# Row maxima of an attention kernel: turned on VectorE in 32x32 blocks instead of on TensorE

## The chip, the cores and the metric

The kernel runs on one core of one Trainium2 chip. Its engines are PE (TensorE, matrix products, with PEld for its weight loads), DVE (VectorE), ACT (ScalarE), POOL (GpSimd) and SP (SyncE, which here only issues DMAs). They run in parallel, each through its own queue in order, and meet in semaphores. The metric is the device time of one execution in microseconds (us).

## The reference

A pre-norm transformer layer on x of 4 sequences, 2048 tokens, 256 features, in float32:

```
h = layernorm(x)
Q, K, V = h Wq^T, h Wk^T, h Wv^T         # 16 heads of 16 features, Q and K turned by RoPE
scores = Q K^T / 4, causal mask           # per sequence and head, 2048 x 2048
x = x + (softmax(scores) V) Wo^T
x = x + relu(layernorm(x) w1 + b1) w2 + b2
```

## The kernel before

There are three stages. Stage 1 normalizes, projects and rotates, and writes q and k (float16, in a high and a low part) and v to scratch in HBM. Stage 2 is the attention, and most of the time. Stage 3 projects the attention's output and does the feed-forward part.

Stage 2 has 16 iterations (4 sequences by 4 groups of 4 heads). An iteration walks 40 steps. A step is one block of 128 keys against one chunk of 512 queries for all 4 heads: chunk 0 has steps 0 to 3, chunk 1 steps 4 to 11, chunk 2 steps 12 to 23, chunk 3 steps 24 to 39. The last four steps of each chunk (0 to 3, 8 to 11, 20 to 23, 36 to 39) lie on the causal diagonal, and their score tiles are 512, 384, 256 and 128 queries wide.

The softmax needs a maximum per query, and since the scores are computed transposed (keys on partitions), the kernel puts minus the maximum in as an extra row (row 48 of each head's 64) of the score product's moving operand `aq`. So each step has two kinds of products:

- Score tiles (L723): one per head, from `ak` and `aq`. ACT takes their exponential into `prob` (L868), POOL zeroes the part above the diagonal in diagonal steps (L898), and PE multiplies with v (L742), one step later.
- Max pairs (L706): two per step, each of two heads. They are approximate scores the other way round, from `mq` and `mk`, half an iteration (LAG = 20 steps) ahead of use. DVE reduces them along the row: one reduction for a full pair (L797), one masking reduction per head on the diagonal (L804). They use four PSUM banks in turn, so that a pair can be written while the pair before it is read.

When the last max pair of a chunk has been read, its row maxima are made ready. This happens in step 24 (for chunk 0 of the next iteration), step 0 (chunk 1), step 4 (chunk 2) and step 20 (chunk 3). DVE reduces the partial maxima to 128x16 (L812), PE transposes them to 16x128 (L714) into a PSUM bank of the max pairs, two uses of the bank ring being counted for it, DVE scales and casts them out (L819), and SP issues four DMAs (L619) that copy them into the four rows of `aq`. PE waits for these rows at the start of steps 0, 4, 12 and 24 (L762). So between the making and the use of the rows lie 16, 4, 8 and 4 steps.

SP's queue in an iteration i is in this order: store of the last output chunk of i-1 (L626, which waits for ACT), rows of chunk 1 (L619), the operands `aq` and `ak` of i+1 (L107, 12 DMAs) and v (L610), rows of chunk 2, sums (L632), two stores, reciprocal sums (L637), the max operands of i+2 (L96, 8 DMAs), rows of chunk 3, a store, rows of chunk 0 of i+1. DMAs of one queue share their engines in order.

In the last 20 steps of the last iteration there are no max pairs left to do.

Of the kernel before, what the change touches and what calls it, by code (L numbers as in the profile page):

```python
# [523 lines left out]
def stage2(nc, x, qk_d, v_d, att_d, rinv_d, weight_ds, weights, ops):  # L524
    with ExitStack() as ctx:
# [6 lines left out]
        ident, mask = ops.ident, ops.mask  # L532
# [3 lines left out]
        qmax = sb("s2_qmax", [P, NC, G * TPC], F32)  # L536
        nrow = sb("s2_nrow", [G * TPC, NC, P], F16)
# [30 lines left out]
        def rows_after(t):

            return [(t // NS, c) for c in range(NC) if t % NS == MAX_END[c]] if t % NS else \  # L570
                [(t // NS - 1, c) for c in range(NC) if t > 0 and MAX_END[c] == NS]

        rows_before = [0]
        for t in range(STEPS_M + 1):
            rows_before.append(rows_before[-1] + len(rows_after(t)))

        def m_use(t, j):

            return G * t + j + ROWS_TILES * rows_before[t]

        def rows_use(i, c):

            t = NS * i + MAX_END[c]
            return G * min(t + 1, STEPS_M) + ROWS_TILES * (rows_before[t] + rows_after(t).index((i, c)))

# [14 lines left out]
        RANK = [sum(e < MAX_END[c] for e in MAX_END) for c in range(NC)]  # L600

# [674 lines left out]
```

## Time and profile before

| | |
|---|---|
| median of 3 runs | 2168.51 us (2166.9 to 2168.56) |
| the profiled execution | 2172.91 us, of it 2171.2 us span from first to last instruction |
| PE busy | 2008.1 us (92%), mean granted clock 0.967 |
| DVE busy | 1902.2 us (88%) |
| ACT, POOL busy | 1457.4 us (67%), 637.1 us (29%) |
| stage 2 | about 227 to 1753 us |

The profiled execution is 4.4 us above the median. A busy PE is not PE at its peak, since its products are pipelined and their ends are modelled: what a step costs on PE is better read from the start of its first product to the start of the next step's. A granted clock of 1.00 is 2.4 GHz, 0.50 is 1.2 GHz.

### The profile page before, as it was taken

The page shows a single profiled execution, that of the slowest core. Times are in us where ns is not written, and L with a number is a line of the kernel's source. Part 1 is how long each engine was busy: PE and PEld are TensorE (multiplying, and loading weights), DVE is VectorE, ACT ScalarE, POOL GpSimd, SP SyncE. Part 2 cuts the span into 40 slices and gives each one's busy share as a digit, 9 for nine tenths or more (in the row PEclk, how much of TensorE's full clock was granted, in tenths as well). Part 3 has the DMA queues.
Part 4 walks back from the last instruction along what each step waited for, and adds up shares of the span by engine and source line. Part 5 has one row for each costly group of instructions (what it writes and reads, how often), then busy time and mean ns, then how long its engine had stood idle before and what let it go on. Part 6 is the DMA issues. An engine that isn't in the chain of part 4 may idle for free. (4 is left out here: it accounts for less than half of the span.)

```text
span 2171.2 us, 53576 instructions
## 1 busy us (share of the span) xinstructions
PE 2008.1 (92%) x19136; PEld 790.4 (36%) x19136; DVE 1902.2 (88%) x3974; ACT 1457.4 (67%) x3092; POOL 637.1 (29%) x1265
## 2 busy tenths in 40 slices
PE   5786599999999999999999999999999969999999
PEld 3444122222222222222222222222222237766776
DVE  8998899999999999999999999999999337777775
ACT  5664078888888788888888788888887742333222
POOL 7999421120221202221121211212212123332231
PEclk9999599999999999999999999999999889999999
DMA  5567331230313303033130322303120212222220
GB/s 193 203 220 209 122 70 37 51 65 17 72 27 64 61 22 66 21 76 50 33 66 17 76 35 52 66 17 74 27 52 13 69 39 78 82 94 84 87 78 29
DMA packets 126407, 152.64 MB, mean 70 GB/s; under 512 B 17248, under 2 KB 92512, under 8 KB 125920
## 3 DMA queue, kind: packets, MB, share of 16 engines
q1 hardware_dynamic: 126176, 149.67, 26.0%
q8 instruction: 132, 2.16, 0.4%
q14 instruction: 99, 0.81, 0.1%
HBM read 90.12 MB, written 59.24 MB: 69 GB/s over the span
## 5 line engine op out<-in xcount | busy, mean ns | idle before, releaser
L868 ACT ACTIVATE s_prob<-s_ps 128x512 f32<-128x512 f32 (+3 forms) x2560 | 1179.3, 540 | 276.5 <-PE s_ps L723 267.3
L797 DVE TENSOR_REDUCE s_part<-s_ps 128x2 f32<-128x1024 f32 x768 | 909.1, 1222 | 42.7 <-PE s_ps L706 25.1
L742 PE MATMUL s_ps<-s_prob,s_v 128*32 128x256 f32 (+3 forms) x10240 | 744.4, 363 | 8.4 <-POOL s_prob L898 0.9
L723 PE MATMUL s_ps<-aq,ak 64*128 64x512 f16 (+3 forms) x2560 | 674.5, 355 | 7.2 <-DVE s_part L804 1.2
L706 PE MATMUL s_ps<-mk,mq 64*128 64x512 f16 (+3 forms) x2560 | 590.7, 355 | 60.4 <-DVE s_part L797 28.1
L898 POOL TENSOR_SCALAR_AFFINE_SELECT s_prob<-s_prob 128x128 f32<-128x128 f32 x1024 | 286.7, 292 | 1170.7 <-ACT s_prob L868 1158.2
L804 DVE CUSTOM_DVE_ANT_0 s_ps<-s_ps,mask_sb 128x512 f32<-128x512 f32 (+3 forms) x1024 | 472.3, 520 | 25.9 <-PE s_ps L706 20.6
L723 PEld LDWEIGHTS s_ps<-aq,ak 64*128 64x128 f16 x2560 | 180.9, 93 | 524.0 <-ACT s_prob L868 439.9
L742 PEld LDWEIGHTS s_ps<-s_prob,s_v 128*32 128x32 f32 x10240 | 202.2, 108 | 464.4 <-issue 378.3
L706 PEld LDWEIGHTS s_ps<-mk,mq 64*128 64x128 f16 x2560 | 141.0, 95 | 105.4 <-DVE s_part L797 48.9
L1166 ACT ACTIVATE s_h_f<-s_ps,s_b_s 128x512 f32<-128x512 f32 x128 | 87.9, 687 | 105.9 <-PE s_ps L1031 85.0
L804 DVE DVE_READ_ACCUMULATOR2_ANT s_part<- 128x1 f32 x1024 | 145.3, 142 | 0.2
L1041 PE MATMUL s_ps<-w_hi,s_h_hi 128*128 128x256 f16 x512 | 139.6, 273 | 2.0 <-DVE s_h_lo L1106 2.0
L1041 PE MATMUL s_ps<-w_hi,s_h_lo 128*128 128x256 f16 x512 | 139.6, 273 | 0.0
L1041 PE MATMUL s_ps<-w_lo,s_h_hi 128*128 128x256 f16 x512 | 139.6, 273 | 0.0
L1106 DVE TENSOR_TENSOR s_h_lo<-s_h_f,s_h_hi 128x512 f16<-128x512 f32 x128 | 100.0, 781 | 4.4
L140 POOL TENSOR_TENSOR o_in<-o_in,r_in 128x1024 f32<-128x1024 f32 x16 | 38.0, 2376 | 202.9 <-DMA r_in<-rinv_scratch 202.9
L445 POOL TENSOR_TENSOR s_rot_b<-s_rot_b,s_sin 128x512 f32<-128x512 f32 x64 | 92.8, 1450 | 14.0 <-DVE s_rot_b L384 13.9
L447 POOL TENSOR_TENSOR s_rot_a<-s_rot_a,s_rot_b 128x512 f32<-128x512 f32 x64 | 93.7, 1463 | 5.0
L1104 DVE CAST s_h_hi<-s_h_f 128x512 f16<-128x512 f32 x128 | 61.8, 483 | 30.2 <-ACT s_h_f L1166 24.9
L1031 PE MATMUL s_ps<-s_xt_hi,w_hi 128*128 128x512 f16 x256 | 77.1, 383 | 2.7 <-DVE s_xt_lo L1099 2.6
L321 PE MATMUL s_ps<-s_xt_hi,s_w_hi 128*128 128x512 f16 x128 | 43.6, 427 | 38.1 <-DVE s_xt_lo L376 33.6
(86 smaller groups left out, 1562.1 us busy)
## 6 DMA issues: line engine op xcount, KB each, us to landing
v_scratch<-s_vst SPq DMA_DIRECT2D x32, 512.0 KB, 3.9
s_v<-v_scratch SPq DMA_DIRECT2D x16, 1024.0 KB, 10.8
att_scratch<-s_o SPq DMA_DIRECT2D x64, 256.0 KB, 2.4
aq<-qk_scratch SPq DMA_DIRECT2D x96, 128.0 KB, 4.3
ak<-qk_scratch SPq DMA_DIRECT2D x96, 128.0 KB, 6.9
s_xin<-x SPq DMA_DIRECT2D x16, 512.0 KB, 4.4
qk_scratch<-s_r_lo SPq DMA_DIRECT2D x64, 128.0 KB, 2.2
qk_scratch<-s_r_hi SPq DMA_DIRECT2D x64, 128.0 KB, 2.4
```

Of the source, the lines that this page charges most:

```text
L445: nc.gpsimd.tensor_tensor(rot_b[:, g], rot_b[:, g], sin[:, tok], ALU.mult).then_inc(rotsin_done, 1)
L447: nc.gpsimd.tensor_tensor(rot_a[:, g], rot_a[:, g], rot_b[:, g], ALU.add).then_inc(rot_done, 1)
L706: nc.tensor.matmul(ps[:, bank_of(use + jj), 0:w], mq[rows, p, pair, qt * P:(qt + 1) * P], mk[rows, p, pair, kc * CH:kc * CH + w], start=Tr ...
L723: nc.tensor.matmul(ps[:, s_bank(s, j), q0:CH], ak[rows, p, j // 2, kb * P:(kb + 1) * P], aq[rows, p, j // 2, c * CH + q0:(c + 1) * CH], st ...
L742: last = nc.tensor.matmul(ps[32 * j:32 * j + 32, O_BANK, cols], v[:, p, kb, j, :], prob[:, s % 2, j, cols], start=kb == 0 and part == 0, s ...
L797: nc.vector.tensor_reduce(part[:, qt // TPC, :, pair, qt % TPC, kc], ps[:, bank_of(use):bank_of(use) + 2, 0:w], AX.X, ALU.max).then_inc(m_ ...
L804: nc.vector.tensor_tensor_reduce(out=ps[:, bank, 0:w], in0=ps[:, bank, 0:w], in1=mask[:, CH - w:CH], scale=1.0, scalar=MASKED, op0=ALU.add ...
L868: nc.scalar.activation(prob[:, s % 2, j, q0:CH], ps[:, s_bank(s, j), q0:CH], ACT.Exp, scale=1.0 / (SQK * DK ** 0.5)).then_inc(p_done, 1)
L898: nc.gpsimd.affine_select(out=block, in_=block, compare_op=ALU.is_ge, fill=0.0, base=0, pattern=[[1, P]], channel_multiplier=-1).then_inc( ...
L1041: last = nc.tensor.matmul(ps[:, Y_BANK + pair, t * D:(t + 1) * D], a[:, p, k, tt * P:(tt + 1) * P], w[:, k], start=q == 0, stop=q == len(m ...
L1106: nc.vector.tensor_tensor(h_lo[:, p, f], h_f[:, f % 2], h_hi[:, p, f], ALU.subtract).then_inc(hlo_done, 1)
L1166: nc.scalar.activation(h_f[:, f % 2], ps[:, H_BANK + f % 2], ACT.Relu, bias=b1_s[:, f:f + 1], scale=SH / SQK).then_inc(h_done, 1)
```

## The change

The transpose leaves PE and PSUM. `qmax` becomes 128x32 per chunk (its columns 16 to 31 are set to zero once), and DVE turns it in four 32x32 blocks, each in its own 32 partitions, within SBUF (`turn_chunk`, new). The turned maxima of 128 queries stand then in four groups of 16 partitions with 32 queries each, and not in 16 partitions with 128. DVE does reduction, turn and scaling one after the other, between the two max pairs of a step, and each waits for the one before. SP waits for `nrow_done` and issues eight DMAs for a chunk, each for 32 of every 128 queries and two heads: 8 partitions of 64 bytes into one row of `aq`. For this `aq` is laid out with the chunk outside the head pair, so that the eight pieces lie at one step, and its load from scratch becomes twelve DMAs of 64 KB in pieces of 1 KB, where it was six of 128 KB in pieces of 4 KB.

The second part is in the last 20 steps of the last iteration. In the eight diagonal ones of them, PE computes two pairs of products 512 wide into the banks of the max pairs (`filler_pair`, new), which nobody reads; before the first of these 20 steps it waits until DVE has read all max pairs.

```diff
@@ load_a
-                dst = (ops.ak if qk else ops.aq)[rows, p]
-                src = qk_d[...].rearrange("a (jp jj r) t -> (a jj) r jp t", jj=2, r=DK)
-                sp.dma_start(dst, src[jj]).then_inc(ops.a_in[p], 16)
+                src = qk_d[...].rearrange("a (jp jj r) t -> (a jj) r jp t", jj=2, r=DK)[jj]
+                if qk:
+                    sp.dma_start(ops.ak[rows, p], src).then_inc(ops.a_in[p], 16)
+                    continue
+                for jp in range(NP):
+                    sp.dma_start(ops.aq[rows, p, :, jp], src[:, jp].rearrange("r (c t) -> r c t", c=NC)
+                                 ).then_inc(ops.a_in[p], 16)
@@ stage2, sync: rows
-                sp.wait_ge(m_read, NM + rows_use(i, c) + ROWS_TILES)
-                for j in range(G):
-                    row = HROWS * (j % 2) + MAXROW
-                    k = TPC * (NP * (j % 2) + j // 2)
-                    sp.dma_start(aq[row:row + 1, i % 2, j // 2, c * CH:(c + 1) * CH], nrow[k:k + TPC, c, :]
-                                 ).then_inc(rows_in[c], 16)
+                sp.wait_ge(nrow_done, NC * i + RANK[c] + 1)
+                for jj in range(2):
+                    row = HROWS * jj + MAXROW
+                    dst = aq[row:row + 1, i % 2, c].rearrange("a n (q u x) -> a u (n q) x", u=P // TURN, x=TURN)
+                    for u in range(P // TURN):
+                        k = TURN * u + NP * TPC * jj
+                        sp.dma_start(dst[:, u], nrow[k:k + NP * TPC, c, :]).then_inc(rows_in[c], 16)
@@ stage2, tensor
-            def max_rows(i, c):
-                use = rows_use(i, c)
-                pe.wait_ge(qmax_done, NC * i + RANK[c] + 1)
-                pe.wait_ge(m_read, use + ROWS_TILES)
-                nc.tensor.transpose(ps[0:G * TPC, bank_of(use), 0:P], qmax[:, c, :], ident[:]
-                                    ).then_inc(m_ready, ROWS_TILES)
+            def filler_pair(p, s, pair):
+                qt, kc = MAX_TILES[(s + LAG) % NS]
+                for jj in range(2):
+                    rows = slice(HROWS * jj, HROWS * (jj + 1))
+                    nc.tensor.matmul(ps[:, M_BANK + 2 * pair + jj], mq[rows, p, pair, qt * P:(qt + 1) * P],
+                                     mk[rows, p, pair, 0:CH], start=True, stop=True)
...
+                    if t == STEPS_M:
+                        pe.wait_ge(m_read, NM + m_use(STEPS_M, 0))
...
+                    elif is_diagonal(s):
+                        filler_pair(p, s, 0)
@@ stage2, vector
+            def turn_chunk(i, c):
+                dve.wait_ge(qmax_done, NC * i + RANK[c] + 1)
+                nc.vector.transpose(qmax_t[:, c, :], qmax[:, c, :]).then_inc(turned, 1)
...
-                nc.vector.tensor_scalar(nrow[:, c, :], ps[0:G * TPC, bank_of(use), 0:P], -1.0 / SQK, None, ALU.mult
-                                        ).then_inc(m_read, ROWS_TILES)
+                nc.vector.tensor_scalar(nrow[:, c, :], qmax_t[:, c, :], -1.0 / SQK, None, ALU.mult).then_inc(nrow_done, 1)
...
-                    for of, c in rows_after(t):
-                        max_of_chunk(of, c)
+                for i, c in ended(t):
+                    max_of_chunk(i, c)
+                    turn_chunk(i, c)
+                    rows_out(i, c)
```

The order of DVE's instructions in step 0, before (L804 are the masking reductions and their accumulator reads, L812 the reduction of a chunk, L819 the scaling):

```order
L804 ISA s_part 128x1
L812 TENSOR_REDUCE s_qmax<-s_part 128x16 [waits s2_m_read]
L804 ISA s_ps,s_part<-s_ps,mask_sb 128x512 [waits s2_m_ready]
L804 ISA s_part 128x1
L804 ISA s_ps,s_part<-s_ps,mask_sb 128x512 [waits s2_m_ready]
L804 ISA s_part 128x1
L819 TENSOR_SCALAR s_nrow<-s_ps 16x128 [waits s2_rows_in1,s2_m_ready]
```

The same place after the change (L801 masks, L809 reduces, L814 turns, L819 scales):

```order
L801 ISA s_part 128x1
L809 TENSOR_REDUCE s_qmax<-s_part 128x16 [waits s2_m_read]
L814 STREAM_TRANSPOSE s_qmax_t<-s_qmax 128x32 [waits s2_qmax_done]
L819 TENSOR_SCALAR s_nrow<-s_qmax_t 128x32 [waits s2_rows_in1,s2_turned]
L801 ISA s_ps,s_part<-s_ps,mask_sb 128x512 [waits s2_m_ready]
L801 ISA s_part 128x1
```

The scaling has moved ahead of the step's second max pair, behind a new instruction, and waits for DVE itself instead of PE.

SP's queue of one iteration before, from its load of `aq` on:

```order
L107 DMA aq<-qk_scratch 16x2x2048 x6
L107 DMA ak<-qk_scratch 16x2x2048 x6
L610 DMA s_v<-v_scratch 128x16x128
L619 DMA aq<-s_nrow 1x4x128 x4
L632 DMA s_sums<-att_scratch 128x1x64
```

And after it (L110 loads `aq`, L616 copies the rows, L605 loads v):

```order
L110 DMA aq<-qk_scratch 16x4x512 x12
L107 DMA ak<-qk_scratch 16x2x2048 x6
L605 DMA s_v<-v_scratch 128x16x128
L616 DMA aq<-s_nrow 1x8x32 x8
L628 DMA s_sums<-att_scratch 128x1x64
```

Nothing has changed places here, but 17 issues have become 27. PE's queue loses its L714 at the end of steps 0, 4, 20 and 24, and is otherwise as before up to the last 20 steps.

## Rows read from the trace of the kernel before

Columns of a timeline: start us, duration us, engine, line, instruction, output<-inputs, form, count, and in brackets the idle time before it and what ended it. Columns of windows: stretch, its length, busy us (and instructions) of PE, PEld, DVE, ACT and POOL, granted clock of PE, busy share of the DMA engines, GB/s.

**Rows 1.** Timeline of PE: first score products of nine steps of one iteration.
```profile
825.70 0.39 PE L723 MATMUL s_ps<-aq,ak 64*128 64x512 f16 x2
...
834.20 0.39 PE L723 MATMUL s_ps<-aq,ak 64*128 64x512 f16 x2
...
839.70 0.39 PE L723 MATMUL s_ps<-aq,ak 64*128 64x512 f16 x2
...
844.54 0.39 PE L723 MATMUL s_ps<-aq,ak 64*128 64x512 f16 x2
...
852.22 0.39 PE L723 MATMUL s_ps<-aq,ak 64*128 64x512 f16 x2
...
856.97 0.39 PE L723 MATMUL s_ps<-aq,ak 64*128 64x512 f16 x2
...
871.51 0.39 PE L723 MATMUL s_ps<-aq,ak 64*128 64x512 f16 x2
...
880.02 0.39 PE L723 MATMUL s_ps<-aq,ak 64*128 64x512 f16 x2
...
885.51 0.39 PE L723 MATMUL s_ps<-aq,ak 64*128 64x512 f16 x2
```

**Rows 2.** Timeline of PE, end of step 0: the transpose and the wait behind it.
```profile
828.06 0.27 PE L714 MATMUL s_ps<-ident_sb,s_qmax 128*16 128x128 f32 x1 [0.39 <-DVE s_qmax L812]
...
829.33 0.33 PE L706 MATMUL s_ps<-mk,mq 64*128 64x384 f16 x1 [0.32 <-DVE s_part L804]
```

**Rows 3.** Windows while the loads of the next iteration land.
```profile
842.00:844.00 2.00, 2.00 (x24) 0.51 (x21) 2.00 (x2) 1.64 (x4) 0.00 (x0) 1.00 1.03 130
846.00:848.00 2.00, 2.00 (x24) 0.52 (x21) 2.00 (x9) 1.70 (x5) 0.95 (x4) 1.00 1.20 294
```

**Rows 4.** Timeline of DVE: runs of full max pairs, waiting for PE and catching up.
```profile
852.97 12.11 DVE L797 TENSOR_REDUCE s_part<-s_ps 128x2 f32<-128x1024 f32 x10 [0.28 <-PE s_ps L706]
...
865.45 6.90 DVE L797 TENSOR_REDUCE s_part<-s_ps 128x2 f32<-128x1024 f32 x6
```

**Rows 5.** Lines of DVE over the whole span: busy us, mean ns | idle before.
```profile
L812 DVE TENSOR_REDUCE s_qmax<-s_part 128x16 f32<-128x64 f32 x64 | 13.6, 212 | 0.0
L827 DVE RECIPROCAL s_rinv<-s_sums 128x64 f32<-128x64 f32 x15 | 8.1, 543 | 0.0
```

**Rows 6.** Timeline of SP (DMA issues) in the same iteration.
```profile
828.74 0.36 SPq L626 DMA_DIRECT2D att_scratch<-s_o  x1
829.43 2.42 SPq L619 DMA_DIRECT2D aq<-s_nrow  x4
831.90 2.77 SPq L107 DMA_DIRECT2D aq<-qk_scratch  x6
...
837.51 0.62 SPq L610 DMA_DIRECT2D s_v<-v_scratch  x1
838.19 8.94 SPq L619 DMA_DIRECT2D aq<-s_nrow  x4
...
874.22 0.42 SPq L96 DMA_DIRECT2D mk<-qk_scratch  x1
875.25 2.47 SPq L619 DMA_DIRECT2D aq<-s_nrow  x4
```

**Rows 7.** DMA issues, whole span: KB each, median us from issue to landing.
```profile
rinv_scratch<-s_rinv SPq DMA_DIRECT2D x15, 32.0 KB, 1.4
```

**Rows 8.** Windows at two falls of the granted clock.
```profile
1655.00:1660.00 5.00, 4.14 (x36) 1.17 (x36) 4.14 (x15) 3.83 (x9) 2.04 (x7) 0.78 0.14 53
1660.00:1665.00 5.00, 4.91 (x69) 1.66 (x61) 3.90 (x21) 2.78 (x10) 2.46 (x9) 0.88 0.00 0
1715.00:1720.00 5.00, 5.00 (x30) 0.93 (x29) 0.00 (x0) 3.64 (x7) 0.00 (x0) 0.50 0.61 171
```

**Rows 9.** Timeline of PE, last iteration: first score products of steps 25 and 32.
```profile
1710.66 1.29 PE L723 MATMUL s_ps<-aq,ak 64*128 64x512 f16 x3
...
1734.33 0.79 PE L723 MATMUL s_ps<-aq,ak 64*128 64x512 f16 x3
```

More of the change, by code:

```diff
@@ L530, in sem @@
             return ctx.enter_context(nc.semaphore(name))
-        ident, mask = ops.ident, ops.mask
+        mask = ops.mask
+        TURN = 32
         mq, mk, aq, ak, m_in, a_in = ops.mq, ops.mk, ops.aq, ops.ak, ops.m_in, ops.a_in
@@ L535, in stage2 @@
         part = sb("s2_part", [P, NC, 2, NP, TPC, NC], F32)
-        qmax = sb("s2_qmax", [P, NC, G * TPC], F32)
-        nrow = sb("s2_nrow", [G * TPC, NC, P], F16)
+        qmax = sb("s2_qmax", [P, NC, TURN], F32)
+        qmax_t = sb("s2_qmax_t", [P, NC, TURN], F32)
+        nrow = sb("s2_nrow", [P, NC, TURN], F16)
         prob = sb("s2_prob", [P, 2, G, CH], F32)
@@ L566, in stage2, with ended @@
         STEPS_M = NIT * NS
[L568 to L575, printed above, removed]
+        RANK = [sum(e < MAX_END[c] for e in MAX_END) for c in range(NC)]
+        def ended(t):
+            return [(i, c) for i in (t // NS - 1, t // NS) for c in range(NC)
+                    if 0 <= i < NIT and t == NS * i + MAX_END[c]]
         def m_use(t, j):
[L579 to L584, printed above, removed]
+            return G * t + j
         def bank_of(use):
@@ L598, in read_before @@
             return ST * i + last_in_bank + 1
-        RANK = [sum(e < MAX_END[c] for e in MAX_END) for c in range(NC)]
         def crosses_diagonal(qt, kc):
@@ L723, in score_tile @@
                 nc.tensor.matmul(ps[:, s_bank(s, j), q0:CH], ak[rows, p, j // 2, kb * P:(kb + 1) * P],
-                                 aq[rows, p, j // 2, c * CH + q0:(c + 1) * CH], start=True, stop=True
+                                 aq[rows, p, c, j // 2, q0:CH], start=True, stop=True
                                  ).then_inc(s_ready, 1)
@@ L771, in iteration @@
                         max_pair(t, 1)
+                    elif is_diagonal(s):
+                        filler_pair(p, s, 1)
                     value_step(i, p, s, 1)
-                    if t <= STEPS_M:
-                        for of, c in rows_after(t):
-                            max_rows(of, c)
             for t in range(LAG):
@@ L779, in _ @@
                     max_pair(t, pair)
-                for of, c in rows_after(t):
-                    max_rows(of, c)
             for u in range(NIT // 2):
@@ L809, in max_of_chunk @@
             def max_of_chunk(i, c):
[L811 to L813 removed]
+                dve.wait_ge(m_read, NM + m_use(NS * i + MAX_END[c], 0))
+                nc.vector.tensor_reduce(qmax[:, c, 0:G * TPC], part[:, c].rearrange("p j n q k -> p (j n q) k"), AX.X,
+                                        ALU.max).then_inc(qmax_done, 1)
+            def turn_chunk(i, c):
+                dve.wait_ge(qmax_done, NC * i + RANK[c] + 1)
+                nc.vector.transpose(qmax_t[:, c, :], qmax[:, c, :]).then_inc(turned, 1)
             def rows_out(i, c):
[L816 to L817 removed]
+                dve.wait_ge(turned, NC * i + RANK[c] + 1)
                 dve.wait_ge(rows_in[c], 16 * ROWS_DMAS * i)
[L819 to L820 removed]
+                nc.vector.tensor_scalar(nrow[:, c, :], qmax_t[:, c, :], -1.0 / SQK, None, ALU.mult).then_inc(nrow_done, 1)
             def invert_sums(i):
@@ L832, in step @@
                     max_of_pair(t, 0)
-                if t <= STEPS_M:
-                    for of, c in rows_after(t):
-                        max_of_chunk(of, c)
+                for i, c in ended(t):
+                    max_of_chunk(i, c)
+                    turn_chunk(i, c)
+                    rows_out(i, c)
                 if t < STEPS_M:
                     max_of_pair(t, 1)
-                if t <= STEPS_M:
-                    for of, c in rows_after(t):
-                        rows_out(of, c)
             dve.sem_inc(m_read, NM)
             nc.vector.memset(part[:], -3e38).then_inc(part_preset, 1)
+            nc.vector.memset(qmax[:], 0.0).then_inc(qmax_preset, 1)
             dve.wait_ge(ops.const_in, 16)
             dve.wait_ge(part_preset, 1)
+            dve.wait_ge(qmax_preset, 1)
             for t in range(LAG):
```

16 lines of the change are left out of this document (5 added, 11 removed).

## The prediction, made before the changed kernel was run

> **What bounds the kernel now.** I read the timeline of PE first and take the start of a step's first score product as its clock. Steps 0, 4, 6, 8, 12, 14, 20, 24 and 26 of one iteration start at 825.70, 834.20, 839.70, 844.54, 852.22, 856.97, 871.51, 880.02 and 885.51 [rows 1]. The reader is to see two lengths for the same work. Four diagonal steps without a transpose take 852.22 - 844.54 = 7.68 us (8 to 11), with one 8.50 (0 to 3) and 8.51 (20 to 23). Two full steps after a diagonal take 856.97 - 852.22 = 4.75 us without, 5.50 (4, 5) and 5.49 (24, 25) with. So a transpose costs 0.82, 0.75, 0.83 and 0.74 us, 3.14 us an iteration, though its own product is 0.27. The rest is waiting: 0.39 us for DVE's reduction before it, and 0.32 behind it in the next max pair, since the transpose takes a turn of the bank ring [rows 2].
>
> Then DVE and PE in a full stretch: both are shown busy for all of 2.00 us [rows 3]. DVE's runs tell them apart. Ten reductions in a row take (12.11 - 1.22) / 9 = 1.21 us each, and when DVE is late after the reciprocal, six take (6.90 - 1.22) / 5 = 1.14 [rows 4]. DVE can go faster than it goes, so PE sets the pace at 2.42 a step and DVE has 0.15 to spare.
>
> Last the queue of SP [rows 6], since rows of maxima reach PE through it and PE waits for them at steps 4, 12 and 24. None of these waits binds now: steps 4 and 24 start without delay against steps 12 and 8 to 11. How near they are is the question.
>
> **PE.** 64 transposes go. Were nothing else late, 16 x 3.14 = 50 us would come back.
>
> **DVE.** Before, a chunk cost the reduction, 0.21 [rows 5], and a scaling. Now it is reduction, turn, scaling, each waiting for the last. No row shows a turn of 128x32 in SBUF. Nearest below is the reduction, 0.21, nearest above the reciprocal of 128x64, 0.54 [rows 5]; I take 0.2 to 0.25 each for turn and scaling, which are smaller than either, so some 0.65 us between the two max pairs, at most 1.3. The reciprocal already puts 0.5 in between full pairs and DVE catches up by itself. In diagonal steps the second pair of the next step can be 0.1 to 0.3 late. I count nothing for it, because the row DMAs below are later still; if they were not, it would be 2 x 0.2 x 16 = 6 us.
>
> A rule on this: the scaling now reads and writes SBUF, and the Trainium skill (SBUF — State Buffer, Who interferes with whom) says that such a VectorE instruction in a two-port mode needs a port pair that it shares with GpSimd, and that whichever comes second is blocked until the other ends. POOL masks in just these diagonal steps. By it the scaling would be late by up to one mask, which hides in the same place; no row here shows the case.
>
> **SP.** This is where the cost is. Four row DMAs take 2.42 us of issue, 0.605 each with the gap [rows 6]; load issues take 0.46 (six in 2.77) and the last operand load 0.42. The new ones are eight per chunk, of the same kind as the old row DMAs (few partitions into one), so I price them at 0.605. Bounds: 0.40, as the store (0.36 and a gap), and 0.65, as the load of v. The landing of a row DMA is not in the trace. From below it is 1.4 us, as for a small store [rows 7]. From above it is 2.9: the fourth issue starts at about 831.25 and PE starts step 4 unhindered at 834.20 [rows 1, 6]. I take 1.6, near the lower row, which is a transfer as small.
>
> The Trainium skill (DMA: Bandwidth & Descriptors, Why a DMA increments its semaphore by 16 and not by 1) says that a DMA is spread over the largest number up to 16 that divides the slowest dimension of both sides, and that the issuing queue writes the missing counts itself. The rows agree in that the copy with 4 partitions takes longer to issue (0.57) than that with 16 (0.42) [rows 6]. By that rule 8 would still be below 16 and pay it, which speaks for 0.605; without it, each would cost 0.46 and the second rival below would hold.
>
> Step 4, times from the start of step 0: the store is issued at 3.04, rows begin at 3.44 (DVE is ready before), the eighth issue starts 7 x 0.605 later at 7.68 and lands at 9.3. PE would be there at 7.68. Steps 0 to 3 take 9.3 instead of 8.50: +0.8.
>
> Step 12: rows of chunk 1 end at 8.28, then 18 loads of 0.467 (there were 12) to 16.7, v to 17.3. Before, the first row DMA of chunk 2 was held: four took 8.94 us from 838.19, so the other three began at about 845.3. The DMA engines were full at 130 GB/s until then and at 294 after [rows 3, 6]. That is 13.4 us after the first load issue at 831.90. The same bytes at the same rate from 8.28 on give 21.7, seven more issues have the last start at 25.3, and it lands at 26.9. PE would reach step 12 at 9.3 + (852.22 - 834.20) - 0.75 - 0.4 = 26.2, where 0.4 is what PE recovers after a wait because ACT and POOL have caught up (estimate: the short product with v of step 3 leaves 4.35 of PE's work in two steps, against 4.75). So steps 0 to 11 take 26.9 against 26.52: +0.4 in all.
>
> Step 24, from the start of step 20: the eight operand loads end at 874.64 - 871.51 = 3.13, rows begin at 3.17, the eighth starts at 7.41, lands at 9.0, against 8.51 before: +0.5. Steps 24 and 25: -0.74 - 0.4 = -1.1. Steps 12 to 19 as before.
>
> Sum of an iteration: 0.4 + 0.5 - 1.1 = -0.2, over 16: -3 us. The 50 us are spent on SP.
>
> **Granted clock.** In the trace it fell in stage 2 after the thinnest stretches of PE's work. In 1655 to 1665 it was 0.78 and 0.88, so 5 x 0.22 / 0.5 + 5 x 0.12 / 0.5 = 3.4 us at 1.2 GHz [rows 8]; there are three such falls in stage 2 (the others near 740 and 1200), each in or after eight diagonal steps (36 to 39, 0 to 3) with a transpose's gap. Now PE stands still for 1.3 to 1.6 us at the end of such stretches, 32 times (steps 4 and 24). I expect the clock to fall at 20 of them. With PE as the bound, 3.4 us at half clock lose 1.7: 34 us, of which 0.7 x 10 hides before step 12, less three falls of before: +23.
>
> **The tail.** Without max pairs the clock fell after the diagonal steps 20 to 23 and stayed at 0.50 [rows 8]: steps 25 to 31 took 1734.33 - 1710.66 = 23.67 us [rows 9]. After it seven steps take 15.4 (2.2 each, where PE no longer waits for the clock). The unread products keep PE as busy as elsewhere, so I expect this fall to go: -8.3. They cost some 0.5, and the wait for DVE's last reductions 1.2 (one pair): -6.5. Six more issues at the end of stage 1 hide behind a full DMA queue: up to 2.8, I take 1.
>
> Sum: 2172.9 - 3 + 23 - 6.5 + 1 = 2187.4 for a profiled execution, which stood 4.4 above the median; so 2183.
>
> **Rivals.**
> 1. The rows arrive in time and PE's gain stays (faster). If an issue costs 0.42 and a gap, step 4 opens at 3.44 + 7 x 0.45 + 1.4 = 8.0 and the 0.3 of waiting is recovered. Then 2172.9 - 50 + 6 - 6.5 = 2122, at the median 2118. It decides below 0.5 us an issue. For it: plain loads issue in 0.46. Against: the row DMAs themselves never do. 22%.
> 2. The waits come, the clock holds. 2187.4 - 23 = 2164, at the median 2160. For it: of 48 diagonal groups only three fell. Against: none of them had such a standstill. 25%.
> 3. As forecast, with the falls. 43%; 2165 to 2205 on its own.
> 4. Worse: the halved loads of `aq` in 1 KB pieces drain slower than 130 GB/s, or falls are longer. A quarter more for the `aq` half is 1.5 us at step 12 each time, 24 us: 2207 and up to 2228. 10%.
>
> The range is 2114 to 2225. A measurement of this kernel tells 0.2% (4 us) from no change. Faster: all of 1, most of 2 and a little of 3, 0.40; same 0.10; slower 0.50.
>
> **What would show it.** PE idle before step 4 and step 24 with DMA on `aq` as the releaser, 1 to 2 us, and less before step 12; steps 4 and 5 in 4.4 us; row DMAs at 0.57 each, eight in 4.8 us; more stretches below 1.00 in the granted clock; no stretch at 0.50 from 1711 to 1732. I am wrong if steps 0 to 3 take 7.7 us, or if a row DMA issues in 0.4 us, and wrong in the clock if it stays at 1.00 in spite of the waits.

## The result and the profile after

| | before | after |
|---|---|---|
| median | 2167.88 us (2166.9 to 2168.56, 4 runs) | 2280.27 us (2276.73 to 2287.94, 4 runs) |
| ratio, 95% interval | | 1.0524 [1.0492, 1.0555] |
| span of the profiled execution | 2171.2 us | 2275.2 us |
| mean granted clock | 0.967 | 0.934 |

The change made the kernel 5.2% slower, 112 us. "Slower" was the likeliest of my cases, but the forecast was 2183 us and the range ended at 2225: the loss is over seven times the 15 us that I gave it. The chain that I had drawn is there in the trace: row DMAs late on SP, PE standing still for them, the clock falling behind. Nearly every link of it is longer than I priced it.

Where the 104 us of span are, by step starts: up to step 0 of the first iteration +2.6 us; from there to step 19 of the last iteration +107.6 us; from there to the end -6.2 us. So it is the body of stage 2. A usual iteration of before takes 91.8 us; of after they take 97 to 103.

The longest entry in the waits of PE is new (line waited for, us in total, times, longest us):

```profile
PE s_ps L719 <- DMA aq<-s_nrow: 77.2, 42, 3.1
```

The timeline of PE after shows one iteration, first score products of steps 0, 4, 6, 8, 12, 14, 20, 24, 26 and the next 0 (L719 is now the score product). It answers to [rows 1]:

```profile
867.77 0.39 PE L719 MATMUL s_ps<-aq,ak 64*128 64x512 f16 x2
...
877.70 0.60 PE L719 MATMUL s_ps<-aq,ak 64*128 64x512 f16 x2 [1.60 <-DMA aq<-s_nrow]
...
884.90 0.39 PE L719 MATMUL s_ps<-aq,ak 64*128 64x512 f16 x2
...
889.75 0.39 PE L719 MATMUL s_ps<-aq,ak 64*128 64x512 f16 x2
...
898.34 0.39 PE L719 MATMUL s_ps<-aq,ak 64*128 64x512 f16 x2 [0.87 <-DMA aq<-s_nrow]
...
903.10 0.39 PE L719 MATMUL s_ps<-aq,ak 64*128 64x512 f16 x2
...
917.64 0.39 PE L719 MATMUL s_ps<-aq,ak 64*128 64x512 f16 x2
...
927.32 0.39 PE L719 MATMUL s_ps<-aq,ak 64*128 64x512 f16 x2 [1.33 <-DMA aq<-s_nrow]
...
933.14 0.39 PE L719 MATMUL s_ps<-aq,ak 64*128 64x512 f16 x2
...
965.15 0.39 PE L719 MATMUL s_ps<-aq,ak 64*128 64x512 f16 x2
```

The reader is to see three waits for the row DMAs, at steps 4, 12 and 24. Steps 0 to 3 take 9.93 us (8.50 before), 4 to 11 take 20.64 (18.02), 20 to 23 take 9.68 (8.51). Steps 4 and 5 take 7.20 us where they took 5.50 with a transpose, and 4.75 was to be had: a fall of the clock. Steps 12 and 13 take 4.76, as before, so nothing is recovered after a wait.

The timeline of SP in the same iteration answers to [rows 6] (L616 rows, L110 loads of `aq`):

```profile
870.81 0.36 SPq L622 DMA_DIRECT2D att_scratch<-s_o  x1
871.22 5.40 SPq L616 DMA_DIRECT2D aq<-s_nrow  x8
877.00 7.71 SPq L110 DMA_DIRECT2D aq<-qk_scratch  x12
884.75 2.91 SPq L107 DMA_DIRECT2D ak<-qk_scratch  x6
887.71 0.59 SPq L605 DMA_DIRECT2D s_v<-v_scratch  x1
888.34 8.69 SPq L616 DMA_DIRECT2D aq<-s_nrow  x8
...
920.81 5.43 SPq L616 DMA_DIRECT2D aq<-s_nrow  x8
```

A row DMA takes 5.40 / 8 = 0.675 us to issue (forecast 0.605), a load of `aq` 7.71 / 12 = 0.64 (forecast 0.467). The second group of rows takes 8.69 instead of 5.4, since it is held behind the loads as before, but begins 20.6 us after step 0, not 17.3.

Windows after (columns as in [rows 3]): the first in PE's standstill before step 4, the second while the loads of `aq` are issued, the third when those of `ak` follow, the fourth behind step 24.

```profile
876.00:878.00 2.00, 0.40 (x6) 0.12 (x4) 0.46 (x4) 0.00 (x0) 0.45 (x2) 0.94 0.01 1
878.00:880.00 2.00, 2.00 (x16) 0.47 (x12) 1.14 (x1) 1.57 (x3) 0.00 (x0) 0.50 0.36 94
...
886.00:888.00 2.00, 2.00 (x24) 0.47 (x16) 1.94 (x2) 1.64 (x4) 0.00 (x0) 1.00 1.07 188
...
929.00:931.00 2.00, 2.00 (x18) 0.69 (x21) 1.93 (x6) 2.00 (x5) 0.00 (x0) 0.50 0.00 0
```

Before, the first load of `aq` was issued at 831.90 [rows 6], and these are the windows that follow:

```profile
832.00:834.00 2.00, 1.91 (x39) 0.86 (x35) 1.94 (x12) 1.49 (x7) 1.52 (x6) 1.00 0.52 125
834.00:836.00 2.00, 1.93 (x32) 0.61 (x24) 1.66 (x5) 1.49 (x4) 0.63 (x3) 1.00 1.03 131
```

Two things: PE runs at 1.2 GHz right behind a standstill, and the DMA engines are 0.32 to 0.42 busy at 94 to 111 GB/s for the 7.7 us in which `aq` is loaded. Before, they were full at 131 GB/s 2 us after the first load was issued. SP's issuing has become the limit of the load, so that its bytes end later. Read in windows of 5 us, the clock was low for 188 us from 280 us to the end of stage 2, in 34 falls of 3.4, 6.8 or 10.2 us; before for 31 us in 4 falls, 20.5 of them in the tail.

VectorE's part answers to [rows 5] (lines over the whole span, busy us, mean ns | idle before): reduction, turn, scaling.

```profile
L809 DVE TENSOR_REDUCE s_qmax<-s_part 128x16 f32<-128x64 f32 x64 | 13.5, 211 | 0.0
L814 DVE STREAM_TRANSPOSE s_qmax_t<-s_qmax 128x32 f32<-128x32 f32 x64 | 13.5, 212 | 2.2
L819 DVE TENSOR_SCALAR s_nrow<-s_qmax_t 128x32 f16<-128x32 f32 x64 | 11.6, 181 | 2.2
```

The turn costs 0.21 us and the scaling 0.18; I had priced each at 0.2 to 0.25.

### The profile page after: what moved, and what is told of

Its sections match the earlier page's. It is cut to its first block and busy times, and to the rows that moved or that the text cites. A ratio compares the mean times of both kernels' runs of the same rounds, so it can differ in the third digit from the quotient of the medians.

```text
span 2275.2 us, 53866 instructions
## 1 busy us (share of the span) xinstructions
PE 2066.4 (91%) x19104; PEld 802.1 (35%) x19104; DVE 1912.0 (84%) x4039; ACT 1453.2 (64%) x3092; POOL 637.0 (28%) x1265
## 2 busy tenths in 40 slices
DMA packets 143306, 152.69 MB, mean 67 GB/s; under 512 B 24928, under 2 KB 112480, under 8 KB 142816
## 5 line engine op out<-in xcount | busy, mean ns | idle before, releaser
L719 PE MATMUL s_ps<-aq,ak 64*128 64x512 f16 (+3 forms) x2560 | 709.1, 371 | 84.5 <-DMA aq<-s_nrow 77.2
L738 PE MATMUL s_ps<-s_prob,s_v 128*32 128x256 f32 (+3 forms) x10240 | 762.5, 371 | 7.6 <-ACT s_o L858 3.2
L702 PE MATMUL s_ps<-mk,mq 64*128 64x512 f16 (+3 forms) x2560 | 632.6, 374 | 42.3 <-DVEq L839 19.1
L801 DVE CUSTOM_DVE_ANT_0 s_ps<-s_ps,mask_sb 128x512 f32<-128x512 f32 (+3 forms) x1024 | 466.1, 525 | 9.5 <-PE s_ps L702 8.4
L719 PEld LDWEIGHTS s_ps<-aq,ak 64*128 64x128 f16 x2560 | 186.8, 94 | 640.9 <-ACT s_prob L867 474.9
L702 PEld LDWEIGHTS s_ps<-mk,mq 64*128 64x128 f16 x2560 | 152.8, 96 | 82.6 <-DVE s_part L801 31.0
L801 DVE DVE_READ_ACCUMULATOR2_ANT s_part<- 128x1 f32 x1024 | 142.7, 139 | 0.0
L449 POOL TENSOR_TENSOR s_rot_b<-s_rot_b,s_sin 128x512 f32<-128x512 f32 x64 | 92.8, 1450 | 15.6 <-DVE s_rot_b L388 15.5
```

Source lines behind the costliest of these rows:

```text
L449: nc.gpsimd.tensor_tensor(rot_b[:, g], rot_b[:, g], sin[:, tok], ALU.mult).then_inc(rotsin_done, 1)
L702: nc.tensor.matmul(ps[:, bank_of(use + jj), 0:w], mq[rows, p, pair, qt * P:(qt + 1) * P], mk[rows, p, pair, kc * CH:kc * CH + w], start=Tr ...
L719: nc.tensor.matmul(ps[:, s_bank(s, j), q0:CH], ak[rows, p, j // 2, kb * P:(kb + 1) * P], aq[rows, p, c, j // 2, q0:CH], start=True, stop=T ...
L738: last = nc.tensor.matmul(ps[32 * j:32 * j + 32, O_BANK, cols], v[:, p, kb, j, :], prob[:, s % 2, j, cols], start=kb == 0 and part == 0, s ...
L801: nc.vector.tensor_tensor_reduce(out=ps[:, bank, 0:w], in0=ps[:, bank, 0:w], in1=mask[:, CH - w:CH], scale=1.0, scalar=MASKED, op0=ALU.add ...
```

## The experiments

Theory S: SP's queue, with eight row DMAs a chunk and twelve loads, opens steps 4, 12 and 24 late, and the clock falls behind PE's standstills. Theory T: VectorE's chain, or the new order on it, is what costs.

**e1, the row DMAs alone.** Before, each row DMA cut in two (2 partitions of 256 bytes instead of 4), transposes and loads as they were.

```diff
-                    sp.dma_start(aq[row:row + 1, i % 2, j // 2, c * CH:(c + 1) * CH], nrow[k:k + TPC, c, :]
+                    for h in range(2):
+                        q0 = c * CH + h * CH // 2
+                        sp.dma_start(aq[row:row + 1, i % 2, j // 2, q0:q0 + CH // 2],
+                                     nrow[k + TPC // 2 * h:k + TPC // 2 * (h + 1), c, :]
```

> The kernel before (transpose on TensorE, plain load of aq), with each of its four row DMAs per chunk cut in two, so eight per chunk. Theory S (the row DMAs on SP's queue open steps 4, 12 and 24 late): rows begin 3.7 us after step 0, the eighth issue starts 7 x 0.65 later and lands 1.75 after that, so steps 0 to 3 take about 10.1 us instead of 8.5, steps 20 to 23 about 10.1, steps 0 to 11 some 2 us more in all, and the granted clock falls after the waits; in all 60 to 110 us slower, 2230 to 2280. Theory T (the turn on VectorE and the new order of DVE make the change slow): 2168, no change.

Measured: 2220.48 us, ratio 1.024 [1.0216, 1.0264]. 256 more small DMAs on a queue with no change on VectorE or PE cost 52 us. Steps 0 to 3 and 20 to 23 take 9.5 and 9.6 us, 4 to 11 stay at 18.0, and there are eleven falls of the clock. This is S in kind, but less than its 60 to 110 us, since the steps take 9.5 and not 10.1. Over half of the loss of after is missing.

**e2, the loads alone.** Before, with the new layout of `aq` and its twelve loads in pieces of 1 KB, four row DMAs.

```diff
+                for jp in range(NP):
+                    sp.dma_start(ops.aq[rows, p, :, jp], src[:, jp].rearrange("r (c t) -> r c t", c=NC)
...
-        A_DMAS = 2 * 3 * 2
+        A_DMAS = 2 * 3 * (NP + 1)
```

> The kernel before with only the new layout of aq and its load in twelve DMAs of 1 KB pieces; four row DMAs per chunk as before. Theory S: the load keeps SP 3.5 us longer before the rows of chunk 2, which then land at about 24.5 us after step 0, while PE arrives at 26.5: not late, so 2165 to 2175. Rival L (the longer load alone costs): steps 4 to 11 grow by some 2 us, 2200.

Measured: 2175.47 us, ratio 1.0038 [1.002, 1.0056]; step 12 late seven times, 5.0 us in all. The loads alone take up the slack before step 12 and cost 8 us by the ratio, 6.5 by the medians.

**e11, both together.** Before with the edits of e1 and e2, transposes kept.

> The kernel before, transposes kept, with both changes of SP's queue together: eight row DMAs a chunk (e1) and the new layout of aq with twelve loads (e2). Alone they cost 52 and 8 us. Theory G (each gate is the end of one queue, so the two add up only at step 12, where nothing was late in either alone): from the start of step 0, rows of chunk 1 end at 8.0, twelve loads of 0.64 at 15.7, six of 0.485 at 18.6, v at 19.2, rows of chunk 2 are held to about 23.5, five more of 0.56 and a landing of 1.75 give 28.6, where PE comes at 9.5 + 18.0 = 27.5. So 1.1 us more an iteration than e1 and e2 together, and some falls behind it: 2240 to 2255. Rival A (the costs are independent and add): 2225 to 2232, step 12 on time. If instead it is at 2275 or more, SP's queue sets the time of the kernel after whatever PE and VectorE do, and the transposes' 50 us would show nowhere.

Measured: 2264.78 us, ratio 1.044 [1.0382, 1.0498]: 98 us, where e1 and e2 add to 60. Neither number held; G was right in kind, since step 12 is now late nearly every time. Its waits and one iteration of SP:

```profile
PE s_ps L729 <- DMA aq<-s_nrow: 58.9, 44, 2.4
```
```profile
863.26 4.90 SPq L625 DMA_DIRECT2D aq<-s_nrow  x8
868.53 8.47 SPq L110 DMA_DIRECT2D aq<-qk_scratch  x12
...
880.63 7.70 SPq L625 DMA_DIRECT2D aq<-s_nrow  x8
```

So a queue of SP with as many issues as that of after loses 98 of the 112 us, with PE and VectorE as they were. The kernel after has no transposes and is still 15 us slower than e11, though the two intervals just touch. What PE saves before a wait makes the wait longer: 77.2 us of waits against 58.9. Its row DMAs are also dearer, 5.40 us for eight against 4.90 here; the runs don't tell these two apart.

**e3, the order of SP's queue.** After, with rows of chunk 2 ahead of the loads of the next iteration and rows of chunk 3 ahead of the max operands.

```diff
                 rows(i, 1)
+                rows(i, 2)
                 if not last:
                     ...
                     load_v(i + 1, 1 - p)
-                rows(i, 2)
...
+                rows(i, 3)
                     load_m(sp, ops, qk_d, i + 2, p)
-                rows(i, 3)
```

> The changed kernel with SP's queue in another order: rows of chunk 2 ahead of the loads of the next iteration, rows of chunk 3 ahead of the max operands; still eight row DMAs. Theory S: the wait at step 12 goes (steps 4 to 11 in 17.3 us plus what a fall of the clock costs, instead of 20.3), steps 20 to 23 take 9.1 instead of 9.6, the wait of 1.6 us at step 4 stays: 2190 to 2225. Theory T: 2280.

Measured: 2223.73 us, ratio 1.0255 [1.0232, 1.0278]. With rows no longer behind the loads the waits go from 77.2 to 42.6 us, all of them now at steps 4 and 24 (1.5 and 0.9 us in a usual iteration), and 57 us come back. Half of the loss was the place of the rows in the queue, most of it the gate at step 12 and what hangs on it; the rows of chunk 3, also moved, shorten steps 20 to 23 from 9.68 us to 9.28, some 6 us of the 57. The falls went from 34 to 20.

This trace also prices the falls where no gate at step 12 hides them. Steps 4 to 11 take 17.26 us in the one iteration without a fall behind step 4, and 19.3 to 19.9 in the twelve with one of 6.8 us. The start of steps 4 and 12 in one of these (L719):

```profile
857.58 0.57 PE L719 MATMUL s_ps<-aq,ak 64*128 64x512 f16 x2 [1.52 <-DMA aq<-s_nrow]
...
877.29 0.39 PE L719 MATMUL s_ps<-aq,ak 64*128 64x512 f16 x2
```

Over the sixteen iterations that is 32 us, and 15 more lie between step 24 and the next step 4. An iteration without falls would take 92.4 us, 0.6 more than before. So of the 55 us that e3 is behind the kernel before, falls of the clock account for about 47 (by the lengths of steps, in a single trace).

**e4, four row DMAs.** After, with one DMA for both halves of the heads: 16 partitions of 64 bytes into two rows.

```diff
-                for jj in range(2):
-                    row = HROWS * jj + MAXROW
-                    dst = aq[row:row + 1, i % 2, c].rearrange("a n (q u x) -> a u (n q) x", u=P // TURN, x=TURN)
-                    for u in range(P // TURN):
-                        k = TURN * u + NP * TPC * jj
-                        sp.dma_start(dst[:, u], nrow[k:k + NP * TPC, c, :]).then_inc(rows_in[c], 16)
+                dst = aq[MAXROW:MAXROW + HROWS + 1:HROWS, i % 2, c].rearrange("a n (q u x) -> a u (n q) x", u=P // TURN, x=TURN)
+                for u in range(P // TURN):
+                    sp.dma_start(dst[:, u], nrow[TURN * u:TURN * u + G * TPC, c, :]).then_inc(rows_in[c], 16)
```

> The changed kernel with four row DMAs per chunk instead of eight, each of 16 partitions by 64 bytes into two rows of aq; twelve load DMAs and the order as in the change. Theory S: the fourth issue starts 1.9 us after the first, rows are there 7.1 us after step 0 (PE comes at 7.7) and 6.8 after step 20, and those of chunk 2 just in time; no waits, no falls of the clock behind them, and all of PE's 3.1 us an iteration comes back: 2110 to 2130. Theory T: above 2200.

Measured: 2146.41 us, ratio 0.9898 [0.9873, 0.9924], faster than before. This one edit takes away 134 us. Rows of chunk 1 in SP's timeline:

```profile
822.37 2.15 SPq L613 DMA_DIRECT2D aq<-s_nrow  x4
```

2.15 us instead of 5.40; no wait at steps 4 and 24, nine at step 12 (7.6 us). T is refuted as the cause of the loss: turn, chain and order on VectorE are those of after. But I had expected 2110 to 2130. The iteration took 89.9 us at best, not 91.8 - 3.1 = 88.7, and e6 and e10 show why.

**e6, four row DMAs and the order.** e4 with the order of e3, the load of the sums also ahead of the loads.

```diff
                 rows(i, 1)
+                rows(i, 2)
+                if not first:
+                    load_sums(i - 1)
                 if not last:
```

> The kernel after, with four row DMAs a chunk as in e4, and the order of e3: rows of chunk 2, then the sums, ahead of the loads of the next iteration; rows of chunk 3 ahead of the max operands. Theory S: the last waits for rows (7.6 us at nine steps in e4) go, and with them a few stretches behind them: 2134 to 2142, against 2146 of e4, and no more, because in e4 VectorE had no idle time in the diagonal steps 0 to 3, which took 8.27 us and not the 7.68 forecast: its chain of reduction, turn and scaling (0.62 us) is on the path there, 1.2 us an iteration, 19 us in all. Rival T (the turn on VectorE is harmless, and what keeps e4 from the 50 us is all rows): 2115 to 2125, steps 0 to 3 in 7.7.

Measured: 2133.67 us, ratio 0.9848 [0.9833, 0.9863]. No wait for rows is left, no fall between the first iteration and the end of stage 2, and an iteration takes 89.87 us. Step starts 0, 4, 8 and 12 (L716):

```profile
813.41 0.39 PE L716 MATMUL s_ps<-aq,ak 64*128 64x512 f16 x2
...
821.68 0.39 PE L716 MATMUL s_ps<-aq,ak 64*128 64x512 f16 x2
...
831.28 0.39 PE L716 MATMUL s_ps<-aq,ak 64*128 64x512 f16 x2
...
838.94 0.39 PE L716 MATMUL s_ps<-aq,ak 64*128 64x512 f16 x2
```

Steps 8 to 11 take 7.66 us, steps 0 to 3 8.27. The timeline of DVE in step 0 (L798 masks, L806 to L816 the chain) has no idle time in brackets behind its first line, nor has it any for the rest of the four diagonal steps:

```profile
814.19 0.70 DVE L798 CUSTOM_DVE_ANT_0 s_ps<-s_ps,mask_sb 128x512 f32<-128x512 f32 x1 [0.41 <-PE s_ps L699]
...
815.45 0.21 DVE L806 TENSOR_REDUCE s_qmax<-s_part 128x16 f32<-128x64 f32 x1
815.70 0.21 DVE L811 STREAM_TRANSPOSE s_qmax_t<-s_qmax 128x32 f32<-128x32 f32 x1
815.95 0.18 DVE L816 TENSOR_SCALAR s_nrow<-s_qmax_t 128x32 f16<-128x32 f32 x1
816.11 0.70 DVE L798 CUSTOM_DVE_ANT_0 s_ps<-s_ps,mask_sb 128x512 f32<-128x512 f32 x1
```

**e10, a part of the chain off VectorE.** e6 with the scaling on GpSimd, behind its masks of the same step.

```diff
-                nc.vector.tensor_scalar(nrow[:, c, :], qmax_t[:, c, :], -1.0 / SQK, None, ALU.mult).then_inc(nrow_done, 1)
+                nc.gpsimd.tensor_scalar(nrow[:, c, :], qmax_t[:, c, :], -1.0 / SQK, None, ALU.mult).then_inc(nrow_done, 1)
```

> The kernel of e6 with the scaling of the turned maxima on GpSimd, after its masks of the same step, instead of on VectorE. In e6 VectorE had no idle time in steps 0 to 3 (8.27 us against 7.68 of steps 8 to 11 before), so the 0.18 us of the scaling should be on the path twice an iteration. Theory D (VectorE sets the pace in these steps): steps 0 to 3 and 20 to 23 each 0.15 to 0.2 shorter, 8.1, and 5 to 6 us in all: 2128, ratio to before 0.981. Rival (something else sets 8.27, ACT or the bank ring): 8.27 stays, 2132 to 2135. A second rival, slower: rows come later by GpSimd's queue and PE waits at steps 4 and 24 for over 0.3 us: 2140 or more.

Measured: 2130.96 us, ratio 0.9827 [0.9811, 0.9844]. Steps 0 to 3 and 20 to 23 take 8.03 us, 0.24 less each, an iteration 89.4 to 89.5. That is D, 0.45 us in an iteration. From the first step 0 to step 19 of the last iteration its trace is 5.3 us shorter than that of e6. The medians differ by only 2.7 us, with intervals that overlap: the first step 0 of its trace lies 1.8 us later than in e6. That VectorE sets the pace in these steps is shown by the step lengths; that e10 is faster than e6 is likely, not shown.

**e5 and e9, unread products before the waits.** After, with six unread products on PE just before the wait for rows at steps 4 and 24 (e5), or five there and sixteen at step 12 (e9). They write only into banks that the next max pair overwrites.

```diff
+                    if s in (CHUNK_START[1], CHUNK_START[3]) and t < STEPS_M:
+                        pe.wait_ge(m_read, m_use(t, 0) + 2)
+                        for k in range(6):
+                            ...
+                            nc.tensor.matmul(ps[:, bank_of(m_use(t, 0) + k % 2)], mq[rows, t // NS % 2, 0, 0:P],
+                                             mk[rows, t // NS % 2, 0, 0:CH], start=True, stop=True)
                     if s in CHUNK_START:
                         pe.wait_ge(rows_in[STEPS[s][0]], 16 * ROWS_DMAS * (i + 1))
```

> The kernel after, with six unread products of 512 columns (1.3 us) on PE just before its wait for the rows at steps 4 and 24. The waits are left as they are; PE only does not stand still in them. It tells the price of the clock's falls from the price of the waits. Theory S (rows late on SP, and each standstill of PE after thin diagonal steps lets the clock fall): the falls, 31 in the kernel after, go to under 8, and the steps of a no-fall iteration stay at 95.9 us against 91.8 before; time 2215 to 2235, against 2280. Rival W (the falls have another cause, or cost nothing because they lie in time that is waited for anyway): 2270 to 2290, with 25 or more falls.

> The kernel after, with unread products of 512 columns on PE ahead of all three waits for rows: five (1.1 us) at steps 4 and 24, sixteen (3.4 us) at step 12. In e5 the sum of the waits stayed (78 us), but step 12 still opened 20.2 us after step 4, so that PE stood still there for 2 to 4 us and the clock fell behind it instead. Theory S (the gate at step 12 is SP's and fixed; a fall costs only where no gate follows it): with no standstill left, 5 falls or fewer between the first and the last iteration, iterations of 95.9 to 96.5 us, 2230 to 2245 in all, against 2282. Rival W (the falls come for another reason, or products of this kind don't hold the clock): 15 falls or more and 2270 to 2290.

Measured: e5 2282.39 us, ratio 1.053 [1.0511, 1.055]; e9 2259.29 us, ratio 1.0423 [1.0402, 1.0444]. e5 missed: no time came back, as W had it, although the falls went from 34 to 20 and low clock from 188 us to about 147 (17 of them one fall in the tail). Its step 12 tells why:

```profile
1082.17 0.39 PE L719 MATMUL s_ps<-aq,ak 64*128 64x512 f16 x2 [1.14 <-DMA aq<-s_nrow]
...
1102.34 0.39 PE L719 MATMUL s_ps<-aq,ak 64*128 64x512 f16 x2 [2.83 <-DMA aq<-s_nrow]
```
```profile
1095.00:1100.00 5.00, 4.43 (x67) 1.61 (x59) 4.92 (x26) 3.38 (x12) 3.32 (x12) 1.00 1.06 214
1100.00:1105.00 5.00, 2.66 (x24) 0.73 (x24) 1.25 (x2) 2.10 (x4) 0.00 (x0) 0.77 0.19 64
1105.00:1110.00 5.00, 5.00 (x37) 1.02 (x29) 3.66 (x3) 2.81 (x6) 0.00 (x0) 0.55 0.15 56
```

Step 12 opens 20.17 us after step 4, as in after (20.64), whether PE runs fast or slow in between. A fall behind step 4 is time that would have been waited for at step 12; with that fall gone, PE stands still 2.83 us there and the clock falls behind step 12 instead. In e9 eleven falls are left (55 us of low clock) and 21 us came back, which is between S and W: its iterations without a fall are at 95.3 to 97.1 us, near the 95.9 to 96.5 of S, but the products were too short to fill the waits. Products of two heads run beside each other, so that sixteen took 1.90 us and not the 3.4 I had counted, and 51.5 us of waits remained:

```profile
1382.27 1.90 PE L763 MATMUL s_ps<-mk,mq 64*128 64x512 f16 x16
1385.20 0.39 PE L719 MATMUL s_ps<-aq,ak 64*128 64x512 f16 x2 [1.02 <-DMA aq<-s_nrow]
```

So in the kernel after the clock's share is bounded, not measured: at least those 21 us.

**e7 and e8, the unread products of the tail.** e7 is e6 without them and without the wait ahead of them; e8 is before with them in seven of the eight steps.

```diff
-                    if t == STEPS_M:
-                        pe.wait_ge(m_read, NM + m_use(STEPS_M, 0))
...
-                    elif is_diagonal(s):
-                        filler_pair(p, s, 0)
```

> The kernel of e6 without the unread products in the last 20 steps and without the wait for VectorE ahead of them. Theory (the tail's part is worth what was forecast, 6.5 us, and the clock falls there again): 5 to 8 us above e6, granted clock 0.50 for some 20 us near the end of stage 2. Rival (the tail's gain of 6.2 us in the kernel after came from the transposes that are gone, not from the clock): within 2 us of e6.

> The kernel before with unread products in seven of the eight diagonal steps of its last 20 (not in the first, where a transpose is left), and PE's wait for VectorE one step later than in the kernel after. Theory: the fall to 0.50 at 1715 us goes, 5 to 8 us faster, 2160 to 2163, ratio 0.996 to 0.998. Rival (as in e7): within 1 us of before.

Measured: e7 2132.99 us, ratio 0.9844 [0.9829, 0.9859], the same as e6; e8 2167.56 us, ratio 0.9996 [0.9986, 1.0006], no change. The second part of the change is worth nothing that can be measured. Windows of e7, of e8 and of after, behind the last diagonal steps 20 to 23, beside [rows 8]:

```profile
1675.00:1680.00 5.00, 4.50 (x48) 1.31 (x40) 0.00 (x0) 4.54 (x10) 0.58 (x3) 0.88 0.35 93
1680.00:1685.00 5.00, 5.00 (x44) 1.17 (x40) 0.00 (x0) 3.63 (x8) 0.00 (x0) 0.78 0.52 162
```
```profile
1715.00:1720.00 5.00, 5.00 (x33) 0.92 (x29) 0.00 (x0) 3.42 (x7) 0.00 (x0) 0.50 0.65 168
1720.00:1725.00 5.00, 4.99 (x46) 1.23 (x42) 0.00 (x0) 3.95 (x8) 0.49 (x1) 0.88 0.26 100
```
```profile
1820.00:1825.00 5.00, 4.50 (x51) 1.36 (x48) 0.00 (x0) 4.21 (x11) 0.89 (x4) 1.00 0.46 155
```

With the products the clock stays at 1.00 in after and in e6. Without them, e7 has one short fall (3.4 us, from 0.88 and 0.78) and not the 20 us of before, and its way from step 24 to step 39 takes 33.7 us against 33.1 in e6; e6 spends 1.4 us more between steps 19 and 24, on the wait for VectorE and the products themselves.

That e7's fall is short is not due to the missing transposes. In e2, which has the tail of before with its transposes and no unread products, the first score products of steps 25 and 32 and the window of the fall are:

```profile
1718.46 1.28 PE L727 MATMUL s_ps<-aq,ak 64*128 64x512 f16 x3
...
1735.55 0.96 PE L727 MATMUL s_ps<-aq,ak 64*128 64x512 f16 x3
```
```profile
1720.00:1725.00 5.00, 5.00 (x40) 1.02 (x32) 0.00 (x0) 3.93 (x8) 0.00 (x0) 0.66 0.64 168
```

Steps 25 to 31 take 17.09 us there, not the 23.67 of [rows 9], and the fall lasts 3.4 us. In e1 and e11, with the same tail, it lasts 6.8. So the 20.5 us belong to the one execution of before that was profiled. Its mean clock was 0.967, and of the fifteen executions of before that stand beside e7 and e8 only three, of 2172.7 us or more, had so low a clock (0.967 or 0.968); the other twelve, of 2165.3 to 2169.7 us, had 0.969 to 0.972. They have no traces, so that their tails are not shown. Why the clock stayed low for 20 us there is open.

## Why the prediction was wrong

Two steps failed. The first is the price of SP's queue. In the terms of my sum for an iteration, 0.4 + 0.5 - 1.1 = -0.2 us became 3.6 + 1.2 - 0.7 = +4.1: steps 0 to 11, steps 20 to 23, and steps 24 and 25, each without falls. That is +63 us in place of -3. The second is the clock, 23 us in the forecast and, by subtraction, 38 to 44 in the kernel after. The whole by its own steps:

- **Transposes gone, 50 us: 31 where rows are not late.** In e6, which never waits for rows, an iteration is 1.9 us shorter than before and not 3.14. Two full steps behind a diagonal take 4.75 us, but steps 0 to 3 and 20 to 23 save 0.23 us each and not 0.82. This did not make the kernel after slow, since the row DMAs end later still; it would have failed the first rival, which kept all but 6 of the 50 us. "I count nothing for it" was too little: I had seen that VectorE's chain would make the next pairs late and priced it at 6 us if uncovered. The diagonal steps 0 to 3 and 20 to 23 have next to no slack on VectorE, so all of the chain counts: 0.6 us twice an iteration, 19 us. e10 shows it by taking 0.18 away and getting 0.24.
- **Row DMAs at 0.605 us: 0.675 in the kernel after.** Cutting one into pieces did not make it cheaper: 0.605 for 4 partitions, 0.6 for 2, 0.675 for 8 into one row, 0.54 for 16 into two. My upper bound of 0.65 was too low. With a landing of 1.75 instead of 1.6, steps 0 to 3 take 9.93 us, not 9.3, and 20 to 23 9.68, not 9.0.
- **Step 12 at 26.9 us after step 0: 30.6.** This is the term that was mis-sized most. The first load is issued 0.9 us late; the twelve loads take 7.7 us instead of 5.6, since I had priced a load of half the bytes, in twice as many pieces of a quarter of the size, at what a whole one cost; `ak` and v end at 20.5 instead of 17.3. And "the same bytes at the same rate" did not hold: before, the DMA engines were full at 131 GB/s, and now they are 0.32 to 0.42 busy in the first half. So the queue empties 15.3 us behind the first load, not 13.4, and the rest of the rows issues later. That is +3.7 us in this iteration. e3, which takes this gate away, shows its weight with what hangs on it: some 50 us.
- **Recovery of 0.4 us behind each wait: none.** Steps 12 and 13 take 4.76. My estimate let the two steps run by PE's own work alone, where the short product with v saves something. The trace before had shown 4.75 for steps 12 and 13 already [rows 1], without a wait ahead of them: that row was the one to take. The 0.4 us behind step 24 went into the sum and don't exist; those behind step 4 did not bind there.
- **Clock, 20 falls of 3.4 us: 34 falls, more than half of them of 6.8.** All three falls in the body of the trace before were of 3.4, and I took their length for a constant. (The terms as written, 34 - 7 - 3 x 1.7, give 22 and not 23.) What a fall costs depends on the place. Behind step 24 one of 6.8 us lengthens the way to the next step 4 from 46.69 us to 49.1 to 50.4; behind step 12 one of 3.4 makes the next two steps 5.85 us instead of 4.76; behind step 4 it costs nothing that shows as long as step 12 is SP's (from step 4 to 12 the median is 20.6 us in after and 20.7 in e5, where nearly all of these falls are gone), and 2.4 us in e3, where it is not.
- **Tail, -6.5: -6.2 measured, by luck.** e7 and e8 show that the unread products bring nothing. The fall of 20.5 us that they were to remove was in the one execution that I read: in e2, with the tail of before, the way from step 19 of the last iteration to the end is 6.5 us shorter than in the trace of before as well. I also took it off twice, once as this fall and once as the 4.4 us by which that execution stood above the median. A sum that agrees is no proof of its terms.
- **Stage 1, +1: +2.6.** e2, which shares only the loads, begins stage 2 at 272.6 us, as after at 272.8. Single traces of other kernels lie between 270.2 and 273.3, so that about half of this is not told apart from chance.

The sum with the runs' sizes: the parts of an iteration of after that no fall touches are 20.2 us (step 4 to 12), 28.98 (12 to 24) and 46.69 (24 to the next 4), 95.9 in all, against 91.8. That is 4.1 x 15.5 = 63 us; by the five iterations of e9 without falls, 96.3 in the mean, it is 70. The other 38 to 44 of the 107.6 are left for the falls and for what they drag along; this is by subtraction, and e9 shows 21 of them. In e3, whose 20 falls stand in the open, they account for about 47 us.

Of the rivals, the fourth was nearest in kind (loads in small pieces, longer falls), but I had it at 10% and ended it at 2228. I priced the terms one by one at or near the figures of shapes that were not the new ones, and each gate takes the sum of all issues ahead of it.

The rule of the Trainium skill that I had drawn on (DMA: Bandwidth & Descriptors, Why a DMA increments its semaphore by 16 and not by 1) says that a DMA runs on the largest number of engines up to 16 that divides the slowest dimension of both sides, and that the issuing queue writes the missing counts. By it the rows of after run on 8 engines, and those of e4, which go into two rows of `aq`, on 2. The packets under 512 bytes agree: 24928 in after and 21344 in e4, 3584 fewer. The 64-byte pieces are as many in both, and 512 DMAs with 8 completion writes against 256 with 2 make just 3584. I had argued that the missing writes make an issue dearer. The runs don't bear that out: e4 misses 14 of 16 and issues in 0.54 us, after misses 8 and takes 0.675. Loads of `aq` have 16 partitions on both sides and went from 0.46 to 0.64 with the smaller pieces. What sets these times is not shown.

## What to carry to other kernels

- A change that takes work from the bounding engine and gives more, smaller DMAs to a queue has to be priced on the queue: number of issues ahead of each gate times the issue time of just that shape. Here 134 us hung on eight row DMAs for a chunk instead of four.
- The order of a queue is worth as much as its contents: what a step waits for goes ahead of what the next iteration needs (57 us in e3, 13 in e6).
- A single trace of the kernel before can hold a rare event, here a fall of 20.5 us that a second trace with the same tail did not have. What a change is to gain on such an event needs the second trace first.
- Before calling an added chain hidden, look for idle time of its engine in exactly those steps; 88% busy over the span says nothing of the steps with no slack.

## What the runs showed of the hardware

- Issue times on one queue, with the gap: 0.46 to 0.51 us for loads from HBM in pieces of 4 KB into 16 partitions, 0.64 to 0.76 for the same partitions in pieces of 1 KB; 0.54 to 0.675 for copies of rows within SBUF.
- In stage 2 the granted clock fell to 1.2 GHz for 3.4, 6.8 or 10.2 us, and in the tail once for 20.5 (before) and once for 17.1 (e5). In the kernel after each of the 34 falls began at or behind a wait for rows of 1.2 us or more. In e3 it fell behind all fifteen waits at step 4, of 1.5 to 3.0 us, and behind two of the twelve waits at step 24 of 0.9 to 1.0 us. In e6, without such waits, it did not fall once in fifteen iterations; before, it fell three times in step 1 with no such wait.
- Products of 64 rows on either half of the array ran beside each other: sixteen of 512 columns in 1.90 us.
